# One step of a cross-attention loop: keys split around the transposes, mixing in two runs, scores from the odd banks

## What is computed

```
xn = layernorm(x, ln_x_g, ln_x_b)             # the context, 1601 rows
ln = layernorm(latents, ln_l_g, ln_l_b)       # 64 rows
q  = (ln @ Wq)                                # 16 heads x 64
kv = concatenate([xn @ Wkv, ln @ Wkv], axis=1)# 1665 keys
qn = rmsnorm(q, qn_g) * scale
kn = rmsnorm(k, kn_g)
sim = einsum('bhid,bhjd->bhij', qn, kn)       # then the mask
attn = softmax(sim)
out = einsum('bhij,bhjd->bhid', attn, v)
return out @ Wout + bout
```

## Time and profile before

| | us |
|---|---|
| median of 3 runs | 2858.78 (2855.47 to 2859.79) |
| the profiled execution | 2861.53, its span 2859.7 |
| layer 0's cross-attention in that span | about 0 to 1140 |
| one step of its loop (from one L1945 to the next) | 16.52 |
| TensorE busy / VectorE / ScalarE / GpSimd, whole span | 91% / 58% / 39% / 21% |

### The profile page before, as it was taken

The page is one execution under the profiler, slowest core; times in us unless marked ns, Lnnn a source line. Parts: engine busy times, 40 slices in busy tenths (PEclk is TensorE's granted clock), DMA queues, the critical chain, the costliest instruction groups (busy, mean ns, idle before and its releaser), DMA issues. The chain is left out here.

```text
span 2859.7 us, 44159 instructions
## 1 busy us (share of the span) xinstructions
PE 2606.5 (91%) x17643; PEld 1795.1 (63%) x17643; DVE 1652.3 (58%) x3730; ACT 1110.6 (39%) x2061; POOL 612.2 (21%) x316
## 2 busy tenths in 40 slices
PE   6999999999999999789999987898987779799978
PEld 3566666666666666557676744454983348688846
DVE  5657566766666554545666655983552450177755
ACT  3343434344343432215555547751332423211123
POOL 2040312122131400000000003981001150145402
PEclk8999999999999999889999998998998899899989
DMA  5324333333323321032010000115868348543210
GB/s 173 96 62 122 76 102 96 82 100 85 100 72 103 82 50 37 28 142 82 24 46 26 1 7 30 54 38 208 325 224 297 122 156 293 191 151 137 70 40 11
DMA packets 88146, 296.07 MB, mean 104 GB/s; under 512 B 9088, under 2 KB 46662, under 8 KB 81030
## 3 DMA queue, kind: packets, MB, share of 16 engines
q1 hardware_dynamic: 83942, 284.27, 31.0%
q0 software_dynamic: 2976, 8.13, 0.8%
q10 hardware_dynamic: 1024, 0.86, 0.1%
HBM read 281.16 MB, written 11.54 MB: 102 GB/s over the span
## 5 line engine op out<-in xcount | busy, mean ns | idle before, releaser
L1962 PE MATMUL L_xattn_bank<-L_xattn_keys_tok,L_xattn_probsT 128*128 128x257 f32 x1664 | 413.4, 392 | 1.1 <-ACT L_xattn_probsT L1781 0.2
L1891 PE MATMUL L_xattn_wide<-L_xattn_keys_feat,weights_a 128*128 128x512 f32 (+2 forms) x1024 | 390.1, 524 | 6.5 <-ACT L_xattn_keys_feat L1801 3.6
L1962 PEld LDWEIGHTS L_xattn_bank<-L_xattn_keys_tok,L_xattn_probsT 128*128 128x128 f32 x1664 | 301.2, 190 | 91.3 <-issue 40.9
L1891 PEld LDWEIGHTS L_xattn_wide<-L_xattn_keys_feat,weights_a 128*128 128x128 f32 x1024 | 186.8, 192 | 155.2 <-issue 129.0
L1539 DVE COPY L_xattn_k_normed<-L_xattn_wide 128x833 f32<-128x833 f32 (+1 forms) x128 | 131.1, 1024 | 189.9 <-PE L_xattn_wide L1891 189.1
L1775 ACT ACTIVATE L_xattn_scores<-L_xattn_scores,L_xattn_neg_max 128x897 f32<-128x897 f32 x128 | 126.4, 1035 | 257.2 <-DVE L_xattn_neg_max L1564 257.2
L3096 POOL TENSOR_TENSOR L_attn_state<-L_attn_state,L_attn_C_rows 128x1024 f32<-128x1024 f32 x80 | 190.4, 2414 | 26.7 <-DVE L_attn_state L2985 25.2
L1559 DVE CUSTOM_DVE_ANT_0 L_xattn_scores<-L_xattn_wide,L_xattn_mask_row 128x897 f32<-128x897 f32 x128 | 134.9, 1088 | 105.9 <-issue 105.9
L2985 DVE TENSOR_TENSOR_SCAN L_attn_state<-L_attn_decay,L_attn_banks 128x1024 f32<-128x1024 f32 x80 | 176.2, 2262 | 15.2 <-PE L_attn_banks L3191 13.9
L2179 DVE CUSTOM_DVE_ANT_0 L_xattn_scores<-L_xattn_banks,L_xattn_mask 128x512 f32<-128x512 f32 (+1 forms) x256 | 131.4, 570 | 92.0 <-issue 92.0
L3797 PE MATMUL L_ffn_banks<-L_ffn_slot_features,L_ffn_expert_w 128*128 128x128 f32 x1440 | 169.0, 278 | 3.0 <-DVE x_tok L3627 3.0
(11 more groups left out here) (531 smaller groups left out, 4634.6 us busy)
## 6 DMA issues: line engine op xcount, KB each, us to landing
L_xattn_k_scale<-L_xattn_k_scale_rows SPq DMA_DIRECT2D x128, 417.0 KB, 4.9
L_ffn_expert_w<-in_x_L_ffn SPq DMA_DIRECT2D x16, 2056.0 KB, 9.0
L_xattn_ctx_feat<-in_ctx_feat SPq DMA_DIRECT2D x19, 1601.0 KB, 9.9
L_ffn_expert_w<-in_x_L_ffn SPq DMA_DIRECT2D x17, 1024.0 KB, 5.7
L_ffn_expert_w<-in_x_L_ffn SPq DMA_DIRECT2D x15, 1028.0 KB, 5.9
L_xattn_keys_tok<-in_ctx_tok SPq DMA_DIRECT2D x8, 1536.0 KB
L_attn_C_rows<-L_attn_c_rows SPq DMA_DIRECT2D x24, 512.0 KB, 3.7
L_xattn_ctx_tok_and_one<-in_ctx_tok SPq DMA_DIRECT2D x8, 1536.0 KB
```

The costliest lines, as they stand in the source:

```text
L1891: last = nc.tensor.matmul(wide[:, 2 * h + c, 0:n], wk[:, k, p * P:(p + 1) * P], xnT[b % 2][:, k, a:a + n], start=(k == 0), stop=(k == KT - 1))
L1962: last = nc.tensor.matmul(bS[:, 0:D + 1], pT[:, c, a, :, :].rearrange("p h q -> p (h q)"), xn[b % 2][:, t, :], start=(i == 0), stop=(i == ...
```

## The change

The second half of the keys is issued in two parts, the 512-column bank ahead of weight groups 2 and 3 and the 320-column bank behind them; the semaphore that reports it goes up after the second part. Mixing tiles 0 to 5 are one run ahead of `means`, so that `apply_v` is followed directly by `scores`. `scores` begins with the odd banks and waits for `key_clamp` only ahead of the even ones. VectorE copies weight group 3 ahead of the second half of the keys.

```diff
@@ vector
                     between(s, 1)
+                    if behind:
+                        weights_turned(s - 1, 3)
                     if ahead:
                         key_copy(s + 1, 1)
-                    if behind:
-                        weights_turned(s - 1, 3)
@@ tensor
-                def keys(s, h):
+                def keys(s, h, parts=range(2)):
                     b, p = divmod(s, NQ)
-                    if s == 0:
+                    first = 0 in parts
+                    if first and s == 0:
...
-                    elif p == 0:
+                    elif first and p == 0:
                         pe.wait_ge(feat_ready, 3 * b)
                     if s == 1 and h == 0:
                         pe.wait_ge(k_clamped, 1)
-                    if s >= 2:
+                    if s >= 2 and first:
                         pe.wait_ge(s_taken, 2 * (s - 2) + h + 1)
                     for c, a, n in banks(h):
+                        if c not in parts:
+                            continue
...
-                    last.then_inc(k_projected, 1)
+                    if 1 in parts:
+                        last.then_inc(k_projected, 1)
@@ scores
                     pe.wait_ge(kn_ready, 2 * s + 2)
-                    if s + 1 < STEPS:
-                        pe.wait_ge(k_clamped, s + 2)
-                    else:
+                    if s + 1 == STEPS:
                         pe.wait_ge(s_taken, 2 * s)
-                    for e in range(2):
+                    for e in (1, 0):
+                        if e == 0 and s + 1 < STEPS:
+                            pe.wait_ge(k_clamped, s + 2)
@@ loop
                     if ahead:
-                        keys(s + 1, 1)
+                        keys(s + 1, 1, range(1))
                     if behind:
                         turn_weights(s - 1, 2)
                         turn_weights(s - 1, 3)
+                    if ahead:
+                        keys(s + 1, 1, range(1, 2))
                     if s >= 2:
                         turn_mixed(s - 2)
                     if behind:
-                        mix(s - 1, range(4))
+                        mix(s - 1, range(6))
                     if ahead:
                         means(s + 1)
                     if s >= 2:
                         apply_v(s - 2)
-                    if behind:
-                        mix(s - 1, range(4, 6))
                     if s < STEPS:
                         scores(s)
```

## The result

The changed kernel takes 2834.57 us (median of 4 runs, 2832.4 to 2836.47) against 2857.31 for the kernel before in the same comparison: 0.9917 of it, 95% interval 0.9901 to 0.9933, so 22.7 us less. Timed again it took 2837.08 (6 runs) against 2858.99 (11 runs), 0.9924 (0.9906 to 0.9942).

A forecast was written before the change was run, and what follows sets the result against it. The prediction took the loop to be bound by TensorE's queue. 55 steps gaining 0.40 us (22.0) less 7 losing 0.63 (4.4) gave 17.6, so 2858.8 - 17.6 = 2841 us, range 2836 to 2852.

The forecast's parts named there:

- The plain step: Sum of the change's parts on one ordinary loop step: 0.40 us gained, between 0.07 and 0.51.
- Merging the runs: Mixing on TensorE in two runs instead of three: the second run's 0.21 us goes (0.14 to 0.28).
- The wait and the load ahead of mixing: Split keys end mixing's 0.09 us wait for ScalarE's copy and hide the 0.14 weights load: 0.23 gained.
- The pair from the value product to the scores: `apply_v` directly followed by `scores`: shape change taken as costing the same as the one replaced, 0.07 dearer or cheaper possible.
- The wait in the middle of the scores: Clamp wait between odd and even banks in `scores`: nothing to 0.16 us, counted as 0.04.
- Cost nothing: VectorE copying weight group 3 before the second keys: free; if that group were late, `means` late by 0.14 us.
- at least the 0.09: Lower bound for splitting the keys: the wait ahead of mixing goes, gaining 0.09 us a step or more.
- The boundary: The 7 steps with p = 6: each loses 0.63 us, with TensorE standing still for 1.5 us.
- Only the wait goes: Rival: merging mixing runs brings nothing, only 0.09 to 0.23 us a step is left; 2850 to 2858 us, chance 0.10.
- The clamp decides: Rival: even banks in `scores` wait 0.16 us each step, so a step gains 0.28; 2848 us, chance 0.10.
- The clock falls at the boundary: Rival: idle at p = 6 halves TensorE's clock for 3.3 us, costing 1.65 each; 2847 to 2853 us, chance 0.10.
- its slower form: Rival: half clock held longer behind the p = 6 gaps, 7 us each costing 24.5; 2866 us, chance 0.04.

The follow-up runs named there:

- mix_odd: Kernel before with mixing in two runs and odd score banks first, keys in one part, old VectorE order: plain step 16.315 us against 16.518; one run 2847.45 us.
- old_dve: Changed kernel with VectorE's old copy order (second keys first, then weight group 3): plain step 16.313 us against 16.130.
- split_keys: Kernel before with the second keys in two parts and VectorE's new order, mixing in three runs: plain step 16.490 us against 16.518; one run 2855.92 us.
- after_gain: Changed kernel with the first product scaling the next batch's context moved ahead of the keys' norm at p = 6: 2823.81 us, 0.9876 of the kernel before.
- before_gain: Kernel before with after_gain's move, and mixing's two extra waits at p = 1 taken ahead of the second keys: 2851.57 us against 2860.1.

## Why the prediction was right, and where it was not

*The plain step.* Forecast 0.40, measured 0.388. Merging the runs: 0.21 forecast, 0.20 in mix_odd. The wait and the load ahead of mixing: 0.23 forecast, 0.19 measured, 0.09 of it the wait and 0.10 the load; I had put 0.14 ahead of a run and 0.07 behind it, and the single records give 0.10 and 0.09. The pair from the value product to the scores, which stood nowhere, costs what the pair before did (0.34 and 0.33). The wait in the middle of the scores costs nothing (1.66 us either way); I had counted 0.04. That 0.40 and 0.388 lie so close is partly luck, since the 0.04 too much ahead of mixing and the 0.04 counted for that wait cancel.

*The covers.* "Cost nothing" for VectorE's order held, and its price without cover, put at 0.14 through the averaging, came out as 0.18 through the multiplication (old_dve). The clamp without the new order: "over 0.5 us", measured 0.66. The lower bound of the first part, "at least the 0.09", was wrong as a statement on that part alone: split_keys gave 0.03, because I had reckoned the cover of the square (0.7) with the two moved tiles already in front of it.

*The boundary.* Forecast a loss of 0.63 and 1.5 us of idle, measured 0.64 and 1.51, through ScalarE's chain behind the clamp, which starts 0.64 later behind the exchange of maxima (11.24 us instead of 10.60); after_gain and before_gain take it away.

*Steps 2 to 62* gave 17.8 us; the sum forecast 17.6 for steps 1 to 62. That the two agree so closely is partly luck: the plain steps gave 0.7 less (55 x 0.012), the steps with p = 1 gave 7 x 0.175 = 1.2 more. This term was missing: I never read a step with p = 1 on TensorE, only on VectorE.

*The step that failed* is the last one, from the sum to the median and its range. I subtracted 17.6 from the median shown, 2858.78, and let the range hold only the bounds of the loop. Nothing stood for the median's own scatter, nor for the 1840 us outside the loop. The measured 2834.57 lies 6.6 us below that sum. Of these, 1.5 are the starting point (2857.31 in the comparison), 0.2 the steps, and 4.9 come from outside steps 2 to 62. That part took 1842.2 and 1840.5 us in the profiles of the kernel before, 1830.8 and 1835.8 in those of the changed one. In the second timing 4.1 us come from there, and its median, 2837.08, lies inside the range by 1.1. That this share is chance alone isn't shown, nor that it belongs to this change; its cause stays open.

*The rivals.* "Only the wait goes" fell with mix_odd (0.20 from merging alone): the new pair doesn't bring back what the second run lost at its ends. One argument against this rival was empty: that both short runs leave the same 0.21 was put in when the pace was taken from their difference; the single records show it (0.32 at the start and 0.31 at the end of both). The rule named there (the Trainium skill, "TensorE: Matmul & The Clock Gate", "Step-by-step: what each phase is for", that TensorE pulls weight loads ahead of products in flight when their row groups don't conflict or the load goes to the background weight buffer) agrees with the trace where the tile shape stays and no wait holds the load, and not where the shape changes, by those 0.20; whether its condition was met there no run shows. "The clamp decides" fell: no cost in the scores, though with a margin of only 0.2 us (the clamp ends at 333.77, the odd part, reckoned at 0.71, at 333.98). "The clock falls at the boundary" and its slower form fell: 1.00 behind all seven gaps of about 1.5 us.

## What to carry to other kernels

In a step whose bound engine is always busy, compare the starts of like runs of different length: what is left after the pace of one record is the cost of a run, and merging two runs saves one such cost (here 0.20 us). The pace is best read from single records. Moves that look worthless can need one another: the new bank order and the split keys were worth 0.00 and 0.03 us alone, but 0.66 and 0.19 with the rest. What comes later in the step must be followed to the next place without cover (here the batch boundary, where moving one product into ScalarE's idle time gave another 11 us a run), and the range must hold the scatter of the whole program, not of the changed part alone.

## What the runs showed of the hardware that I had not expected

Two waits whose signals had come long before cost 0.175 us in the kernel before, where they stood directly ahead of the first load of a run, and nothing where they stood ahead of the second keys (before_gain), nor in the changed kernel, where they stood as before. And one stretch of later work takes 59.4 us in one profile of the changed kernel and 61.9 in the other with the same instructions, at a mean granted clock of 0.92 and 0.87 (the two levels, 1.2 and 2.4 GHz, averaged).
